# Layer 1's expert weights, gate weights and last attention sums handed from the softmax stage to the experts' block

## The reference, cut to what matters

```python
xn = _layernorm(x)
x = x + _L0_attn_ref(xn, ...) + _L0_ffn_ref(xn, ...)     # sigmoid attention; 32 experts of 64, one shared
xn = _layernorm(x)
x = x + _L1_attn_ref(xn, ...) + _L1_ffn_ref(xn, ...)     # softmax attention with relative positions
# _L1_ffn_ref: 16 experts of 176 columns, top 4 of 2 groups, and a shared one of 352
combine_w = (one_hot(topk_idx, E) * topk_w[..., None]).sum(1)
act = silu(einsum('th,eih->tei', x, gate_proj)) * einsum('th,eih->tei', x, up_proj)
y = einsum('tei,ehi,te->th', act, down_proj, combine_w) + (silu(x @ sg.T) * (x @ su.T)) @ sd.T
```

## Time and profile before

| what | value |
|---|---|
| median of 3 runs | 1197.96 us (1195.48 to 1201.27) |
| the profiled execution, device time | 1194.37 us |
| its span in the trace | 1192.6 us |
| PE / DVE / ACT / POOL busy, share of the span | 86% / 63% / 61% / 45% |
| softmax stage | about 403 to 932 us of the span |
| experts of layer 1 | 932 us to the end |

### The profile page before, as it was taken

The page is one execution under the profiler, slowest core; times in us unless marked ns, Lnnn a source line. Parts: engine busy times, 40 slices in busy tenths (PEclk is TensorE's granted clock), DMA queues, the critical chain, the costliest instruction groups (busy, mean ns, idle before and its releaser), DMA issues. The chain is left out here.

```text
span 1192.6 us, 22324 instructions
## 1 busy us (share of the span) xinstructions
PE 1026.4 (86%) x7844; PEld 648.4 (54%) x7844; DVE 755.5 (63%) x1671; ACT 729.6 (61%) x1096; POOL 540.1 (45%) x723
## 2 busy tenths in 40 slices
PE   1499999999996548999999999999998178999997
PEld 1344444777774524554555555455544156878785
DVE  6145241677876247787788888777771056676766
ACT  1289988555553126777777777777765065555453
POOL 1166776465553130444434333333223187655554
PEclk9999999999998557999999999999999599999999
DMA  5521231644563297888888888888740554433443
GB/s 132 227 85 53 64 119 45 150 121 137 164 187 107 98 257 246 246 239 242 243 238 242 241 243 238 244 244 243 224 139 11 169 168 120 124 116 121 116 122 94
DMA packets 147132, 197.42 MB, mean 166 GB/s; under 512 B 34361, under 2 KB 113562, under 8 KB 146970
## 3 DMA queue, kind: packets, MB, share of 16 engines
q1 hardware_dynamic: 125868, 184.98, 50.8%
q0 software_dynamic: 21152, 11.01, 5.6%
HBM read 123.00 MB, written 72.74 MB: 164 GB/s over the span
## 5 line engine op out<-in xcount | busy, mean ns | idle before, releaser
L977 ACT ACTIVATE a_probs<-a_duo 128x1024 f32<-128x1024 f32 x256 | 261.7, 1025 | 80.5 <-PE a_duo L910 79.6
L1376 POOL TENSOR_TENSOR f_hid_lo<-f_hid,f_hid_hi 128x512 fp32r<-128x512 f32 (+1 forms) x168 | 216.6, 1291 | 147.6 <-ACT f_hid_hi L1347 147.6
L826 POOL DMA_DIRECT2D scr_y1c<-ys x256 | 126.7, 504 | 252.4 <-DVE ys L1005 240.1
L1029 DVE TENSOR_REDUCE a_part<-a_duo 128x2 f32<-128x1024 f32 (+3 forms) x256 | 215.5, 855 | 12.2 <-PE a_duo L885 10.8
L1022 DVE CUSTOM_DVE_ANT_0 a_band_sum<-a_duo,a_rel_raw 128x256 f32<-128x256 f32 (+2 forms) x320 | 131.4, 448 | 87.8 <-PE a_duo L885 58.2
L973 ACT ACTIVATE a_rel<-a_rel_ps 128x384 f32<-128x384 f32 x246 | 120.3, 489 | 55.4 <-PE a_rel_ps L872 39.3
L636 ACT ACTIVATE a_probs<-a_duo 128x1024 f32<-128x1024 f32 x192 | 139.7, 830 | 21.5 <-PE a_duo L585 20.1
L925 PE MATMUL a_acc_ps<-a_probs,a_v 128*32 128x256 f32 x2048 | 143.7, 387 | 0.1
L872 PE MATMUL a_rel_ps<-emb_all,a_q 31*128 31x384 f32 x247 | 112.8, 457 | 28.9 <-ACT a_rel L973 11.6
L574 POOL TENSOR_TENSOR a_probs<-a_probs,const 128x256 f32<-128x256 f32 x128 | 100.1, 798 | 58.4 <-ACT a_probs L636 58.1
L1495 DVE TENSOR_TENSOR f_u<-f_u,f_gate 128x512 f32<-128x512 f32 (+1 forms) x100 | 69.7, 697 | 86.6 <-PE f_u L1250 45.5
(11 more groups left out here) (235 smaller groups left out, 1932.5 us busy)
## 6 DMA issues: line engine op xcount, KB each, us to landing
scr_rel<-a_rel SPq DMA_DIRECT2D x128, 384.0 KB, 3.8
a_rel_raw<-scr_rel SPq DMA_DIRECT2D x128, 384.0 KB, 4.5
w_share<-scr_cw SPq DMA_DIRECT2D x128, 128.0 KB, 3.2
f_share<-scr_cw SPq DMA_DIRECT2D x40, 256.0 KB, 3.2
scr_y1c<-ys POOLq DMA_DIRECT2D x256, 8.0 KB, 3.7
f_raw<-in_w SPq DMA_DIRECT2D x21, 192.0 KB, 3.3
f_share<-scr_cw SPq DMA_DIRECT2D x20, 192.0 KB, 2.9
f_share<-scr_cw SPq DMA_DIRECT2D x16, 224.0 KB, 3.0
```

Of the source, the lines that this page charges most:

```text
L826: pool.dma_start(scr["y1c"][w, b, head, :, at:at + QUARTER], ys[32 * (2 * hd + c) + HD * w:32 * (2 * hd + c) + HD * (w + 1), h % 2, :]).th ...
L977: act.activation(probs[:, n % KEPT, :], bank_pair("t", n)[:], ACT.Exp, scale=SCALE).then_inc(exp_done, 1)
L1029: ins = dve.tensor_reduce(part[:, h % 2, x, :, j % 4], both[:, :, lo * P:hi * P], AX.X, ALU.max, negate=True)
L1376: pool.tensor_tensor(hid_lo[0:m, n % 4, :], hid[0:m, n % 2, :], f32(hid_hi[0:m, n % 4, :]), ALU.subtract).then_inc(lo_ready, 1)
```

## The change

- `Weights` of layer 1 is made with 7 early chunks and with its shares. POOL, in its loop over pairs in the softmax stage, loads the 7 chunks in three pieces (one for each matrix, 128 x 896) into a free part of `cwT` and splits each piece itself, one piece after each of the pair steps 8, 9 and 10. The 18 other chunks are 6 groups of 3 in the experts' block, split in steps 1, 4, 7, 10, 13 and 16; groups 0 and 1 are loaded at its start, group 2 in step 4.
- `probs` takes 4 of its 6 slots in `xn` and `yT`.
- `cw` is turned in the loop: for the halves 23 to 30 DVE copies two tiles of `cw` (34 columns) beside the 8 maxima into `joint` (128 x 72), the one transpose (L956 before) turns all of it, and DVE makes a second copy, of 34 rows, from PSUM to `cwT`. PE waits for that copy too before the next slot. The 16 transposes and 4 ACT copies at the end are gone.
- SP stores `cw` after its loop with 2 transfers, then the sums of half 30 (8 transfers), and then issues the shares of chunks 0 to 3, all still in the softmax stage.
- POOL stores the sums of halves 0 to 29 only. Those of half 31 are stored by SP in the experts' block, after the loads of groups 0 and 1, and the wait for all sums asks for them in a third semaphore.

```diff
+def y_store(sb, scr, eng, saved, h, done):
+    pair, x = h // 2, h % 2
+    if saved is not None:
+        eng.wait_ge(saved, h + 1)
+    for hd in range(2):
+        for c in range(2):
+            b, head = pair // (H // 2), 2 * pair % H + hd
+            at = x * (T // 2) + c * (T // 4)
+            for w in range(2):
+                eng.dma_start(scr["y1c"][w, b, head, :, at:at + T // 4],
+                              sb["ys"][...]).then_inc(done, 16)
...
+    TURN, STEP = 23, weights.early * P
...
-        probs = tile("probs", [P, KEPT, T])
+        more = tile("probs", [P, KEPT - 4, T])
+        probs = [flat(sb["xn"])[:, 0:T], flat(sb["xn"])[:, T:2 * T], sb["yT"][:, 0:T], sb["yT"][:, T:2 * T]] + [more[:, i, :] for i in range(KEPT - 4)]
...
+        stage = [sb["cwT"][:, NB * P:NB * P + STEP]]
...
-            weights_stored(router, sb, scr, sp)
+            sp.wait_ge(router.cw_saved, NB)
+            for i in range(2):
+                sp.dma_start(scr["cw"][0:L1.E + 1, :].rearrange(...)[i], sb["cwT"][...]).then_inc(router.cw_stored, 16)
+            y_store(sb, scr, sp, y_saved, 2 * PAIRS - 2, y_stored[2])
+            sp.wait_ge(router.cw_stored, 32)
+            for n in range(SHARES):
+                share_out(weights, scr, sp, weights.share, n)
...
             for pair in range(4, PAIRS + 4):
-                store(2 * (pair - 4))
+                if pair < PAIRS + 3:
+                    y_store(sb, scr, pool, y_saved, 2 * (pair - 4), y_stored[0])
...
-                store(2 * (pair - 4) + 1)
+                if pair < PAIRS + 3:
+                    y_store(sb, scr, pool, y_saved, 2 * (pair - 4) + 1, y_stored[1])
                 if pair - 2 < PAIRS:
                     copy_v(pair - 2)
+                if pair >= 8:
+                    for _ in range(2 if pair == 8 else 1):
+                        next(loading, None)
+                    for _ in range(2):
+                        next(splitting, None)
...
                 if (m - 3) % 8 == 7 and 0 <= m - 3 < SLOTS:
                     pe.wait_ge(row_saved, (m - 3) // 8 + 1)
+                    wait(pe, router.cw_saved, min((m - 3) // 8 + 1 - TURN, NB))
...
-                    pe.transpose(max_rows, negmax[...], ident).then_inc(row_ready, 1)
+                    pe.transpose(joint_rows, joint[:, h % 2, :], ident).then_inc(row_ready, 1)
...
-            weights_turned(router, sb, pe, banks)
...
-            weights_saved(router, sb, act, banks)
...
+                        if 0 <= h - TURN < NB:
+                            if h == TURN:
+                                dve.wait_ge(router.cw_ready, 1)
+                            then(dve.tensor_copy(joint[:, h % 2, 0:2 * (L1.E + 1)].rearrange("p (t e) -> p t e", t=2),
+                                                 router.cw[:, 2 * (h - TURN):2 * (h - TURN) + 2, :]))
...
+                    dve.tensor_copy(rows_sb[64:72, h % 2, :], max_rows).then_inc(row_saved, 1)
+                    if 0 <= h - TURN < NB:
+                        at = (h - TURN) * P
+                        dve.tensor_copy(sb["cwT"][0:2 * (L1.E + 1), at:at + P], shown).then_inc(router.cw_saved, 1)
...
             if k == 1:
+                y_store(sb, scr, sp, None, B * H - 1, y_stored[2])
                 sp.dma_start(wp[:], d["wproj"]).then_inc(small, 16)
...
-        weights = Weights(nc, ctx, L1, 0, False)
+        weights = Weights(nc, ctx, L1, 7, True)
...
-        experts(nc, d, sb, scr, L1, weights, y_stored[1], (128 * H, 128 * H))
+        experts(nc, d, sb, scr, L1, weights, y_stored[1], (128 * (H - 1), 128 * (H - 1), 256))
```

More of the change, by code:

```diff
@@ L692, in softmax_attention @@
         band_sum = tile("band_sum", [P, 2, 2, BAND])
-        negmax = tile("negmax", [P, 2, 2, 4])
-        rows_sb = tile("rows", [8, 2, P], F32R)
+        joint = tile("joint", [P, 2, 72])
+        rows_sb = tile("rows", [72, 2, P], F32R)
         ys = sb["ys"]
@@ L700, in softmax_attention @@
         ident = sb["const"][:, C_ID:C_ID + P]
-        max_rows = rel_ps[0:8, BAND:BAND + P]
+        joint_rows, max_rows = rel_ps[0:72, BAND:BAND + P], rel_ps[64:72, BAND:BAND + P]
         cleared, step, ones_ready = sem("cleared"), sem("step"), sem("ones_ready")
@@ L752, in band @@
             return max(j - 1, 4 * x), min(j + 2, 4 * x + 4)
-        banks = [duo[c // 2][:, c % 2 * CH:(c % 2 + 1) * CH] for c in range(NC)]
+        shown = rel_ps[0:2 * (L1.E + 1), BAND:BAND + P]
+        stage = [sb["cwT"][:, NB * P:NB * P + STEP]]
         block = ctx.enter_context(nc.Block())
@@ L794, in _ @@
                         sp.dma_start(f32(qs[to:to + 1, home(pair), x * HALF:(x + 1) * HALF]),
-                                     f32(rows_sb[4 * hd:4 * hd + 4, h % 2, :])).then_inc(row_stored[h % 2], 16)
-            weights_stored(router, sb, scr, sp)
+                                     f32(rows_sb[64 + 4 * hd:68 + 4 * hd, h % 2, :])).then_inc(row_stored[h % 2], 16)
+            sp.wait_ge(router.cw_saved, NB)
+            for i in range(2):
+                sp.dma_start(scr["cw"][0:L1.E + 1, :].rearrange("e (t i p) -> i e t p", i=2, p=P)[i],
+                             sb["cwT"][(L1.E + 1) * i:(L1.E + 1) * (i + 1), 0:NB * P].rearrange("e (t p) -> e t p", p=P)).then_inc(router.cw_stored, 16)
+            y_store(sb, scr, sp, y_saved, 2 * PAIRS - 2, y_stored[2])
+            sp.wait_ge(router.cw_stored, 32)
+            for n in range(SHARES):
+                share_out(weights, scr, sp, weights.share, n)
         @block.gpsimd
@@ L816, in load @@
                 pool.dma_start(f32(dst[rows(pair, hd, K3), home(pair), :]), scr[name][:, 2 * pair + hd]).then_inc(qk_reloaded[pair % 4], 16)
[L818 to L827, removed]
             pool.wait_ge(first_loaded, 96)
@@ L835, in _ @@
             copy_v(1)
+            loading, splitting = weights_loaded(weights, d, pool, stage, STEP), weights_split(weights, pool, stage, STEP)
             for pair in range(4, PAIRS + 4):
                 done = 16 * (pair - 4)
-                store(2 * (pair - 4))
+                if pair < PAIRS + 3:
+                    y_store(sb, scr, pool, y_saved, 2 * (pair - 4), y_stored[0])
                 if pair < PAIRS:
@@ L924, in values @@
                         at = hd * CH + c * QUARTER
-                        ins = pe.matmul(acc[to:to + 32, 0:QUARTER], vs[:, pair % 2, hd, kt, :], probs[:, n % KEPT, at:at + QUARTER],
+                        ins = pe.matmul(acc[to:to + 32, 0:QUARTER], vs[:, pair % 2, hd, kt, :], probs[n % KEPT][:, at:at + QUARTER],
                                         start=(n % 8 == 0), stop=(n % 8 == NB - 1))
@@ L955, in _ @@
                     wait(pe, saved_dve, dve_n)
-                    pe.transpose(max_rows, negmax[:, h % 2, :, :].rearrange("p a b -> p (a b)"), ident).then_inc(row_ready, 1)
+                    pe.transpose(joint_rows, joint[:, h % 2, :], ident).then_inc(row_ready, 1)
                 if n >= 0:
@@ L976, in _ @@
                     wait(act, pv_done, n + 1 - KEPT)
-                    act.activation(probs[:, n % KEPT, :], bank_pair("t", n)[:], ACT.Exp, scale=SCALE).then_inc(exp_done, 1)
-            weights_saved(router, sb, act, banks)
+                    act.activation(probs[n % KEPT], bank_pair("t", n)[:], ACT.Exp, scale=SCALE).then_inc(exp_done, 1)
         @block.vector
@@ L997, in _ @@
             dve.wait_ge(part_filled, 1)
+            then(dve.memset(joint[:], 0.0))
             for n in slots:
@@ L1034, in _ @@
                         wait(dve, row_ready, h - 1)
-                        dve.tensor_reduce(negmax[:, h % 2, :, :].rearrange("p a b -> p (a b)"),
+                        if 0 <= h - TURN < NB:
[3 more added lines that the diff above has]
+                                                 router.cw[:, 2 * (h - TURN):2 * (h - TURN) + 2, :]))
+                        dve.tensor_reduce(joint[:, h % 2, 64:72],
                                           part[:, h % 2, :, :, :].rearrange("p k a b -> p (a b) k"), AX.X, ALU.min).then_inc(max_ready, 1)
```

2 lines of the change are left out of this document (1 added, 1 removed).

## The result

| | before | after |
|---|---|---|
| median of the runs timed together | 1199.11 us (4 runs, 1195.48 to 1201.27) | 1169.35 us (4 runs, 1165.56 to 1172.71) |
| profiled execution, device time / span | 1194.37 / 1192.6 us | 1172.71 / 1170.8 us |

The ratio is 0.9754 [0.9713, 0.9794]: 29.8 us by the medians, where 29.6 were forecast. The profiled executions differ by only 21.7: that of before lies 4.7 us under its median, that of after 3.4 above. So I compare stage by stage. First the seam, in two views of the changed kernel: the drains at the end of the softmax stage (duration in ns, then start in us), and the timeline (start, duration, engine, in us).

A forecast was written before the change was run, and what follows sets the result against it. PE, busy 86% of the span, bounds the kernel; its idle time can be won. Chunk 24's `hid_lo`: 929.5 + 55.5 + 2 + 3 = 990.0 instead of 1019.63, 29.6 us less: 1168 us, range 1160 to 1178.

The forecast's parts named there:

- The seam: Softmax stage to layer 1's experts: without POOL's late drain SP starts the block at 918.45 instead of 932.55, 14.1 us.
- Rival 3: At the seam: POOL's drain is not tied to its last transfers and ends where it ended; 14.1 us late, 1182; chance 0.04.
- The entry: Start of the experts' block: chunk 1's `hid_lo` at 929.5 instead of 962.90, 33.4 us earlier, 14.1 of it the seam.
- rival 4: In the entry: PE idles, is granted 1.2 GHz, rounds take 11.5 us instead of 7.92; 1186 us, chance 0.02.
- The rounds: Experts' block, chunk 1 to chunk 24: five rounds of 7.92 us and the rest, 55.5 us where it was 56.7.
- the wait: Experts' block: DVE waits for chunk 4's share behind SP's stores and loads; a stall of 2 us, bounds nothing and about 8.
- Rival 1: In the entry: the stall for chunk 4's share is 6 to 8 us; 1173 to 1175 us, chance 0.14.
- The softmax stage: Halves with `cw` copies: DVE's second copy and the copy ahead of the maxima cost 3.0 us in all, bounds 1 and 5.
- The early splits: POOL's 6 splitting operations in the softmax stage: hidden in POOL's idle time, no cost to DVE or PE counted.
- POOL's three steps: Softmax stage: issue 0.5, landing near 4.1, two operations of 2.3 each; 9.2 us per step, hidden in 11.96 us idle.
- rival 5: POOL's queue in the softmax stage: steps over 33 us each delay `ys`; at 47 us each 1210 us; chance 0.04.
- the prediction's bound of 14 us: Softmax stage: most the 6 POOL splitting operations could add if DVE, and PE with it, stood still for them: 14 us.

The follow-up runs named there:

- e1: Kernel before, with the sums of halves 30 and 31 stored by SP inside the softmax block ahead of the store of `cw`: 1193.47 us, ratio 0.9957.
- e4: Changed kernel, but POOL stores half 31's sums at the end of the softmax stage instead of SP in the next block: 1183.42 us, ratio 0.9868.
- the repeat: The changed kernel itself, unedited, timed and profiled once more: 1169.48 us, ratio 0.9747 to the kernel before.
- e7: Changed kernel, but in layer 1's experts' block SP issues a chunk's share before the weight-group load of the same step: 1168.16 us, ratio 0.9771.
- e3: Changed kernel without early chunks, all 25 loaded and split in the experts' block, the rest kept: 1182.57 us, ratio 0.9869.
- e2: Kernel before, with the 7 early chunks alone; shares, `cw` and stores as they were: 1186.17 us, ratio 0.9902.
- e5: Changed kernel, but DVE subtracts the low part of w2 in layer 1's experts' block, POOL those of w1 and w3: 1171.85 us, ratio 0.9781.
- e10: Changed kernel with shares issued before group loads and a weight group split one matrix per step instead of three in one: 1174.94 us, ratio 0.98.
- e11: Changed kernel, shares before loads, one matrix split per step, and the splits and loads two steps later: 1179.53 us, ratio 0.9842.

## Why the prediction was right

**The seam: as forecast (14.1 us).** POOL's drain follows its last issued transfers, shown by e1 (moved away, gone from the path) and e4 (put back: 13.3 us of seam by the profiles, 14.1 us by the medians). Rival 3, a drain that ends where it ended, is refuted. e1 showed also what the working only stated: without the earlier store of `cw` 9.5 of the 14.1 us remain.

**The entry: 19.0 us for 19.3.** ACT's first copy came 4.8 us after SP's first load instead of 4.1, and `hid_lo` of chunk 0 7.2 us after it instead of 6.7; it was the landing and not PE that decided, as said. PE did fall to the lower clock for the chunk that follows (matmuls of 0.63 us from 938.4 to 940.9, 0.40 from 942.1 on), but POOL was in its split of 2.94 us then. The granted clock of the windows 930 to 940 and 940 to 950 is 0.90 and 0.93, where the earlier trace rows had 0.67, so rival 4 did not happen in this execution. In the repeat it was 0.50 from 938 to 942 us.

**The rounds: 57.4 us for 57.5, and the match is luck.** The forecast was 55.5 us and a stall of 2 at chunk 4. DVE waited 8.7 us for shares: 2.98 for chunk 4's, 1.63, 1.44 and 2.44 for those of chunks 7, 10 and 13. Little of it reached POOL, which at chunk 4 lost 0.42 us, since it was still in a split. The 1.9 us over 55.5 are 0.5 in chunk 4's round, 0.9 in the round from chunk 7 to 10, and 0.6 behind chunk 16. The repeat took 59.06 us for the same stretch.

The working of the wait was wrong in several terms that cancelled. SP's list ran as forecast up to `wp`, though its 8 stores took 2.7 us instead of 3.37. The load of group 2 was issued only at 940.5, 2.5 us after the second load of sums: it waits for the split of group 0, which ended at 940.49, and the prediction let it go at once. Against that, the transfers were faster: 406 GB/s from 941 to 945 us, where 302 was the mean of a window with slower parts. The share thus landed at most 18.3 us after SP's first load, where 19.5 were forecast. It was still late, because DVE stood ready for it at 15.3 us and not at 17.5. Nor is the wait for the buffer the main cause: in e7 the share is issued straight behind the sums and is used 17.2 us after SP's first load, only 1.1 us sooner. The rest seems to be the transfers of the sums, which landed 4.9 and 7.0 us after their issue in the change; no run leaves them out. Rival 1, a stall of 6 to 8 us, was not reached.

**The softmax stage: 3.5 us for 3.0, with terms mis-sized.** The copies cost less: 2.1 to 2.4 us, and they fall on every other half (jumps of 0.57 to 0.67 in halves 23, 25 and 27, 0.34 in 29, nothing between). Of the rest 0.9 us lies between half 0 and half 1, where the clock of this execution was still rising (0.80 from 480 to 490 us); in e7, with the same code, there is none of it. The early splits, taken as 0, cost 0.3 us, in half 12. In the 11 profiles with early splits this jump is 0 to 1.1 us, and e1 and e3, which have no splits, don't show it.

The 1.6 us that e2 took more are not the splits: 0.4 of them lie between halves 0 and 1 (e1, without splits, has 0.3), and 1.2 between halves 15 and 16, where the granted clock fell for a while. The repeat of the change has the same dip:

```profile
700.00:710.00 10.00, 9.55 (x80) 5.34 (x82) 6.84 (x20) 5.96 (x10) 5.20 (x11) 0.83 0.96 240
```

The ten profiles with the change's code in this stage took 445.5 to 451.0 us from half 0 to half 31, where before and e1 took 442.5 and 442.8. The longest is e5, with four such dips, three of them in halves that carry a copy. So this stretch took 3.0 to 4.1 us more in seven of the ten, and 5.8, 6.4 and 8.6 in the others, where the clock rose late or dipped. What makes it dip was not tested.

For the copies, the groups of the whole stage in the changed kernel:

```profile
L895 PE MATMUL a_rel_ps<-emb_all,a_q 31*128 31x384 f32 x247 | 114.7, 464 | 30.4 <-ACT a_rel L996 11.6 <-DVE a_rows L1070 9.3 <-DVE a_rel L1033 5.1
L1073 DVE COPY cwT<-a_rel_ps 34x128 f32<-34x128 f32 x8 | 2.3, 283 | 0.2
L980 PEld LDWEIGHTS a_rel_ps<-const,a_joint 128*72 128x72 f32 x32 | 3.7, 115 | 11.5 <-issue 10.5 <-DVE a_joint L1063 0.9
```

and of the kernel before:

```profile
L872 PE MATMUL a_rel_ps<-emb_all,a_q 31*128 31x384 f32 x247 | 112.8, 457 | 28.9 <-ACT a_rel L973 11.6 <-DVE a_rows L1042 7.6 <-DVE a_rel L1010 5.2
L956 PEld LDWEIGHTS a_rel_ps<-const,a_negmax 128*8 128x8 f32 x32 | 2.7, 85 | 11.8 <-issue 10.8 <-DVE a_negmax L1035 1.0
```

The copy of 34 rows takes 283 ns, the 0.28 of the earlier trace rows; PE's wait for the copies of maxima grew by 9.3 - 7.6 = 1.7 us; loading 72 columns costs 30 ns more than 8, in 32 halves 1 us of PE's load queue that lies beside matmuls.

**POOL's three steps: 9.2, 9.1 and 8.4 us for 9.2.** The first of them:

```profile
619.97 0.60 POOL L257 DMA_DIRECT2D cwT<-in_w  x1 [0.53 <-issue]
626.06 0.93 POOL L266 CAST w_w_hi<-cwT 128x896 fp32r<-128x896 f32 x1 [5.50 <-DMA cwT<-in_w]
627.08 2.12 POOL L269 TENSOR_TENSOR w_w_lo<-cwT,w_w_hi 128x896 fp32r<-128x896 f32 x1
629.97 4.02 POOL L673 DMA_DIRECT2D scr_y1c<-ys  x8 [0.77 <-DVE ys L1028]
```

The landing was longer (5.5 for 4.1), the cast shorter (0.93 for 2.3), and 0.77 us of POOL's idle time are left before the next store. The idle cover was thus nearly used up, but behind it stood the two halves until `ys` is needed, and rival 5 was far off.

**The sum.** The cause of the gain, a seam of 14 us and an entry of 19, is as forecast. That the total came out within 1 us is partly luck: the stretches of the profiles give 25.9 to 28.9 us, and the interval of the ratio allows 25 to 34.

## What to carry to other kernels

Here a block whose last transfers were issued by POOL ended with a drain of 9.5 to 11 us: look at which engine is drained last, and give those transfers to SP, at the start of the next block if they are late. Before counting such a gain, list what is late next; here that was a landing 10 us behind the last copy, and only moving both brought the 14 us. Where one queue carries, in order, both large loads that wait for a free buffer and small ones needed each step, a later moment at which the buffer comes free makes the small ones late too, as in e10 and e11. And before a stretch of one profile is put down to an edit, look at the granted clock in it and at the same stretch in other runs with the same code.

## What the runs showed of the hardware

- POOL's drain at the end of a block after transfers it issued took 10.99, 11.00, 11.11, 11.11 and 11.15 us in five kernels, and 9.49 us in e4. It was as long where its last stores were the end of the stage as where they were issued 15 us ahead of PE's end. What fills it was not tried.
- The softmax stage starts at a granted clock of 0.50, and the moment of the rise differed between executions of the same code. PE was 95 to 100% busy by the records in windows that still showed 0.50. Later in the stage it fell again for a while in five of the 14 executions: a half with a mean of 0.89 or 0.90 was 1.2 to 1.6 us longer. Half 0's copy fell between 475.24 and 482.43 us in 14 profiled executions. A single profiled execution can't tell a change of 7 us in this kernel; stretches between two events can, to some 3 us (the change and its repeat).
- POOL and DVE slow each other when both subtract from SBUF: POOL 1.00 to 1.34 us for 128x384 and 1.29 to 1.60 for 128x512, DVE 1.02 to 2.07 us for two of 128x384. In the softmax stage, where DVE mostly reads PSUM, three casts and three subtractions of 896 columns on POOL cost PE at most 1.1 us. This agrees with the rule of the Trainium skill, GPSIMD Engine Reference, section 1, Specifications, that GpSimd contends with VectorE where the latter has two SBUF inputs; the prediction's bound of 14 us by it was not approached.
